# Two transformer layers on one core: merge, norm and routing of the first layer moved into attention, its operands in the weight ring's memory

## The reference, cut to what matters

```python
q, k, v = proj(Wq, bq, layernorm(x)), proj(Wk, bk, ctx), proj(Wv, bv, ctx)   # 16 heads of 16 dims, 256 positions
prob = softmax(einsum("bdhn,bdhm->bhnm", rope(q), rope(k)) / sqrt(16))
x = x + Wm @ einsum("bhnm,bdhm->bdhn", prob, v) + bm
h = layernorm(x)                                   # 1024 tokens of 256
topk_w, topk_idx = top_k(softmax(h @ gate_w.T), 8) # of 64 experts
x = x + sum over the 8 of topk_w * (silu(h @ w1[e].T) * (h @ w3[e].T)) @ w2[e].T
```

## Time and profile before

| | us |
|---|---|
| median of three runs (815.94 to 818.72) | 818.17 |
| the profiled execution's own time | 816.76 |
| its span, first to last instruction | 814.7 |
| busy: TensorE matmul, VectorE, POOL, ScalarE | 477.9, 375.1, 339.5, 206.8 |

### The profile page before, as it was taken

The page is one execution under the profiler, slowest core; times in us unless marked ns, Lnnn a source line. Parts: engine busy times, 40 slices in busy tenths (PEclk is TensorE's granted clock), DMA queues, the critical chain, the costliest instruction groups (busy, mean ns, idle before and its releaser), DMA issues. The chain is left out here.

```text
span 814.7 us, 11260 instructions
## 1 busy us (share of the span) xinstructions
PE 477.9 (59%) x3381; PEld 369.9 (45%) x3381; DVE 375.1 (46%) x1177; ACT 206.8 (25%) x533; POOL 339.5 (42%) x464
## 2 busy tenths in 40 slices
PE   2707997995645000998889920433520499898930
PEld 1602544552533000887778810322320488888820
DVE  8936766670477000343344415688760022222216
ACT  0530756675111000432223201120200122222200
POOL 8564212220047773364455440003054366666610
PEclk9965989998775555899999975655555599999975
DMA  4295478875993333799975318500007199999816
GB/s 156 75 203 111 140 227 258 248 270 180 391 365 156 155 155 126 251 320 320 325 253 173 114 56 308 221 0 20 0 21 203 42 272 289 279 301 293 255 36 254
DMA packets 78736, 159.30 MB, mean 196 GB/s; under 512 B 12267, under 2 KB 47093, under 8 KB 76896
## 3 DMA queue, kind: packets, MB, share of 16 engines
q1 hardware_dynamic: 55776, 109.72, 42.7%
q0 software_dynamic: 13168, 32.02, 11.7%
q10 hardware_dynamic: 9744, 16.98, 5.9%
HBM read 105.05 MB, written 56.12 MB: 198 GB/s over the span
## 5 line engine op out<-in xcount | busy, mean ns | idle before, releaser
L558 DVE TENSOR_REDUCE at_top<-at_ps_top 128x2 f32<-128x512 f32 x128 | 82.6, 686 | 49.2 <-PE at_ps_top L498 48.5
L1507 POOL DMA_INDIRECT rows<-hd_out,hd_rows x64 | 62.2, 972 | 66.6 <-DVE hd_out L1458 43.5
L1031 POOL DMA_INDIRECT held<-e_extended,e_address x64 | 61.9, 968 | 67.1 <-DVE e_address L1023 47.9
L1360 PE MATMUL hd_ps_up<-hd_x_turned,e_w 128*128 128x160 f32 x512 | 84.0, 308 | 0.0
L591 ACT ACTIVATE at_prob<-at_ps_score 128x512 f32<-128x512 f32 x128 | 72.2, 596 | 45.8 <-PE at_ps_score L516 45.4
L1665 PE MATMUL l_ps_up<-l_x_turned,e_up_w 128*112 128x128 f32 x672 | 82.2, 276 | 0.0
L1665 PEld LDWEIGHTS l_ps_up<-l_x_turned,e_up_w 128*112 128x112 f32 x672 | 81.0, 180 | 2.6
L1360 PEld LDWEIGHTS hd_ps_up<-hd_x_turned,e_w 128*128 128x128 f32 x512 | 77.4, 195 | 8.8 <-issue 6.2
L853 POOL DMA_INDIRECT table<-choice,ft_r_address x32 | 30.7, 958 | 111.0 <-DVE ft_r_address L844 102.2
L1495 DVE TENSOR_TENSOR hd_inner<-hd_silu,hd_ps_up 128x160 f32<-128x160 f32 x64 | 20.5, 321 | 119.5 <-ACT hd_silu L1445 118.6
L498 PE MATMUL at_ps_top<-op_k_in,op_q_in 96*128 96x256 bf16 x256 | 54.8, 302 | 23.5 <-PEq L110 21.4
(11 more groups left out here) (280 smaller groups left out, 903.6 us busy)
## 6 DMA issues: line engine op xcount, KB each, us to landing
e_w<-in_weights SPq DMA_DIRECT2D x64, 384.0 KB, 12.1
e_up_w<-in_up SPq DMA_DIRECT2D x42, 448.0 KB, 4.3
held<-at_empty ACTq DMA_DIRECT2D x16, 960.0 KB, 5.4
hd_rows<-held SPq DMA_DIRECT2D x15, 768.0 KB, 10.1
e_down_w<-in_down SPq DMA_DIRECT2D x42, 224.0 KB, 5.6
ft_g_rows<-rows SPq DMA_DIRECT2D x8, 1024.0 KB, 12.5
parts<-op_parts SPq DMA_DIRECT2D x8, 576.0 KB, 7.6
attended<-at_out SPq DMA_DIRECT2D x8, 512.0 KB, 6.4
```

The lines of the kernel that those rows point to most:

```text
L558: nc.vector.reduce_max(top[:, 2 * h:2 * h + 2], ps_top[at % TOPS][:], AX_X).then_inc(top_found, 1)
L1031: self.nc.gpsimd.indirect_dma_start(self.held_dram, to, self.held.extended[:, b, :], None)\
L1360: op = nc.tensor.matmul(ps_up[e % 2][:, part, :], w[:, k, part * P:(part + 1) * P], x_turned[g % 2][:, j, k, :], start=k == 0, stop=k == 1)
L1507: nc.gpsimd.indirect_dma_start(rows_out, to, out_ap, None, bounds_check=TOKENS * LAYER0.chosen - 1, oob_is_err=False).then_inc(semaphore, 16)
```

## The change

The merge block is gone. `attend_phase` gets its work as further steps of the pipeline: batch b's store of the second half is at step 16b + 20, read back (`load_packed`) at 16b + 22, divided at 26, merged at 27, added and normalised at 28 and 29, turned at 31, chosen at 33, ranked at 35; POOL scatters four times from 38 and four times from 46. The loop runs 28 steps past the last head. Storing and reading `attended` transposes the layout, so the sums are not turned on TensorE; the norm is applied by ScalarE. `RowRouting` works on one batch. All of merge and routing share one PSUM bank, and `at_ps_out` has one bank in place of two. `q_in`, `k_in` and `v_in` lie in an `arena` that is the weight ring's memory: ScalarE issues the 32 weight loads, one every second step from step 85, each after the batches that used its place. The emptying of `held` is issued by ScalarE in `project_phase`, 2 MB a batch, and POOL waits for all of it in attention.

```diff
--- before.py
+++ after.py
@@ Operands.__init__
-        self.q = [s.sbuf(f"q_in{n}", [ROWS, H * D], BF16) for n in range(DEEP)]
-        self.k = [s.sbuf(f"k_in{n}", [ROWS, H * D], BF16) for n in range(DEEP)]
-        self.v = s.sbuf("v_in", [P, B, 2, H, VW], F32)
+        halves = arena.bitcast(BF16)
+        self.q = [halves[0:ROWS, 2 * n * H * D:(2 * n + 1) * H * D] for n in range(DEEP)]
...
+        self.v = arena[:, DEEP * H * D:].rearrange("p (b m h v) -> p b m h v", b=B, m=2, h=H)
@@ project_phase, ScalarE, for b in range(B)
                 cut(b, full[n], 0, 3, TERMS).then_inc(high_cut, 1)
                 if b >= 1:
                     cut_mid(b - 1)
+                held.act_empty(act, b)
@@ Held
+    def act_empty(self, act, b):
+        if b == 0:
+            act.wait_ge(self.empty_set, 1)
+            act.dma_start(self.of_dummy, self.empty[:, 0:ROW0]).then_inc(self.emptied, 16)
+        each = GROUPS // B * EACH
+        act.dma_start(self.of_expert[each * b:each * (b + 1)].rearrange("e (p c) -> p e c", p=P),
+                      self.empty[:].unsqueeze(1).broadcast_to([P, each, self.PIECE])).then_inc(self.emptied, 16)
+
+    def pool_wait_emptied(self, pool):
+        pool.wait_ge(self.emptied, 16 * (B + 1))
@@ Rstd.dve_scale, in place of Norm
+        link.free(nc.vector.tensor_scalar(half, variance, EPS, -0.5, ALU.add, ALU.mult))
+        link(nc.vector.tensor_scalar(full, variance, EPS, None, ALU.add))
+        link(nc.vector.tensor_scalar(root.bitcast(I32), full.bitcast(I32), -0.5, float(0x5F3759DF), ALU.mult, ALU.add))
+        for _ in range(NEWTON):
+            link(nc.vector.scalar_tensor_tensor(work, root, half, root, ALU.mult, ALU.mult))
+            link(nc.vector.scalar_tensor_tensor(root, work, 1.5, root, ALU.add, ALU.mult))
+        nc.vector.scalar_tensor_tensor(shift, self.mean_var[:, 0:1], -1.0, root, ALU.mult, ALU.mult).then_inc(ready, 1)
@@ attend_phase, SP
+            def load_packed(b):
+                if b >= 2:
+                    sp.wait_ge(divided, b - 1)
+                for p in (2 * b, 2 * b + 1):
+                    sp.wait_ge(stored[p % 4], 16 * (p // 4 + 1))
+                by_head = attended[b].rearrange("g (j v) n -> (g j) v n", v=VW)
+                for k in range(2):
+                    sp.dma_start(packed[b % 2][:, k, :], by_head[:, k * HD:(k + 1) * HD, :]).then_inc(packed_loaded[b % 2], 16)
@@ attend_phase, POOL
+            operands.set_rows(nc, pool, DEEP - 1)
+            held.pool_wait_emptied(pool)
+            for at in range(-LEAD, END + LEAD):
+                hh, late = divmod(at + LEAD, HALF)
+                if late == HALF - 1 and hh < HALVES:
+                    cut_tops(hh)
+                for k in range(LAYER0.chosen):
+                    b = batch_at(at, SCATTER_AT + k % 4 + k // 4 * HALF)
+                    if b is not None:
+                        routing.pool_scatter(pool, b, k)
@@ attend_phase, VectorE
+            def divide(b):
+                dve.wait_ge(packed_loaded[b % 2], 32 * (b // 2 + 1))
+                link(nc.vector.reciprocal(share[:], packed[b % 2][:, 1, :]))
+                if b >= 1:
+                    dve.wait_ge(merged, b)
+                nc.vector.tensor_tensor(heads[:], packed[b % 2][:, 0, :], share[:], ALU.mult).then_inc(divided, 1)
@@ attend_phase, ScalarE
+                if at >= (DEEP + 1) * H + 4 and at % 2 == 1 and waiting:
+                    e = waiting[0]
+                    if ring.free_after[e] * H + 4 < at:
+                        act.wait_ge(weighted, 4 * ring.free_after[e])
+                        ring.load(act, waiting.pop(0))
```

More of the change, by code:

```diff
@@ new lines, in dve_targets @@
+    def dve_targets(self, dve, link, b):
+        targets = self.held.extended.bitcast(I32)[:, b, D + 1::2]
+        dve.wait_ge(self.mask_ready, b + 1)
+        link.free(self.nc.vector.tensor_tensor_scan(targets, self.consts.ones[:, 0:self.layer.experts], self.held.mask[:, b, :],
+                                                    self.consts.more[:, SLOTS_AT + b:SLOTS_AT + b + 1], ALU.mult, ALU.add))
+        dve.wait_ge(self.expo_ready, b + 1)
+        self.nc.vector.reciprocal(self.share[:], self.total[:]).then_inc(self.share_ready, 1)
@@ L1060, in pe_rows @@
         pe.wait_ge(self.own_ready, 1)
[L1061 to L1062 removed]
+        for n, to in enumerate((self.ps_row[:, 0, :], self.ps_row[:, 1, :], self.ps_block)):
+            last = self.nc.tensor.transpose(to, self.own[:, n:n + 1], self.consts.identity[:])
         last.then_inc(self.rows_ready, 1)
@@ new lines, in _ @@
+            operands.load(sp, DEEP - 1)
+            inputs.load(sp)
+            for at in range(-LEAD, END):
+                hh, late = divmod(at + LEAD - 5, HALF)
+                if late == HALF - 1 and 0 <= hh < HALVES:
+                    place(hh)
+                p, late = divmod(at - HALF - 4, HALF)
+                if late == 0 and 0 <= p < HALVES:
+                    store(p)
+                b = batch_at(at, LOAD_AT)
+                if b is not None:
+                    load_packed(b)
+                b = batch_at(at, H + 4)
+                if b is not None and b + DEEP < B:
+                    sp.wait_ge(weighted, 4 * (b + 1))
+                    operands.load(sp, b + DEEP)
@@ new lines, in weigh @@
+            def weigh(group, half):
+                b, g = group // 4, group % 4
+                if half == 0:
+                    pe.wait_ge(prob_ready, 4 * group + 4)
+                    if group >= 2 and g % 2 == 0:
+                        pe.wait_ge(out_kept, group // 2)
+                for j in range(4):
+                    last = nc.tensor.matmul(ps_out[32 * j:32 * j + VW, g % 2, :], v_in[:, b, half, 4 * g + j, :],
+                                            prob[(4 * group + j) % RING][:, half, :], start=half == 0, stop=half == 1,
+                                            skip_group_check=True)
+                if half == 1:
+                    last.then_inc(weighted, 1)
@@ new lines, in lift_once, with merge @@
+            def lift_once():
+                pe.wait_ge(inputs.loaded, 48)
+                nc.tensor.matmul(ps_merged[:, 0:1], inputs.w[:], inputs.bias[:, 0:1], start=True, stop=True).then_inc(lift_ready, 1)
+            def merge(b):
+                if b >= 1:
+                    pe.wait_ge(routing.rank_read, b)
+                else:
+                    pe.wait_ge(lift_known, 1)
+                pe.wait_ge(divided, b + 1)
+                nc.tensor.matmul(ps_merged, inputs.w[:], heads[:], start=True, stop=True).then_inc(merged, 1)
```

754 lines of the change are left out of this document (332 added, 422 removed).

## The result

The changed kernel took 845.62 us (median of 4 executions, 844.12 to 850.84), the kernel before 818.03 on the same chip: ratio 1.035, 95% interval 1.030 to 1.040. It is slower by 3.5%, where I had forecast 793. The profiled execution took 844.12 us, its span is 842.4; 791.6 had been forecast for it.

What follows compares the result with a forecast made beforehand. After attention, a merge stage waited for addresses and POOL's 81 us of scatters, while POOL and VectorE had spare time in attention. Terms -82.2 + 28 + 24 + 5 = -25 gave 791.6 profiled, median 793, range 762 to 825.

Steps and rivals of the forecast that it cites:

- VectorE's term: Attention steps 20 to 108: VectorE takes on the merge for batches 0 to 4, +24 us, bounds +3 and +40.
- Rival D: Attention: SP's placing comes late behind the half-batch's read-back and TensorE waits, +24 us, no change at 817; chance 0.11.
- my signs: Listed trace signs; wrong if emptying lands by 85, clock sits at 0.5 through a batch, or VectorE idles a quarter of middle.
- The merge stage to tail: After step 132: the 120.1 us merge stage shrinks to a 37.9 us tail for batch 7, -82.2, bounds -87 and -76.
- The emptying, +28: Projection: emptying `held` there delays POOL's first cut of the maxima and step 0 by 28 us, bounds +13 and +36.
- first cut near 98 after the last transfer: Sign at projection's end: POOL first cuts the maxima near 98 us, after the emptying's last transfer, against 70.1 before.
- ScalarE, +5: Attention steps 108 to 132: ScalarE issues 12 weight loads and does routing activations, +5 us, bounds +2 and +9.
- The reciprocal: VectorE's reciprocal of 256 values in each batch's merge, taken as 1.1 us, bounds 0.45 and 2.2.
- C: Rival: repeated TensorE stops in attention keep the clock at its lower level, granted 0.5, 844 us; chance 0.14.
- B: Rival: emptying fits in at +13, VectorE's additions fall in its waits (+3), ScalarE +2; -64, 754 us; chance 0.22.
- E: Rival: scatters don't hide in attention, needing POOL over 19 us a batch; no own chance, others together 0.03.

## Why the prediction was wrong

The forecast for the profiled execution was 791.6, the measurement 844.1, 52.5 more. Of these, 46.4 lie in the middle and late part of attention (175.3 us against 99.9 + 24 + 5 = 128.9), 4.4 in the tail and 2.6 ahead of step 20; what follows `held` took 0.6 less.

**The step that failed: VectorE's term, +24 with bounds +3 and +40.** Its sentence on waits, "nothing to 5 us a batch; I take 2, as each is one cross-engine answer issued in the same step", forgot the one wait that isn't an answer of an engine. The round trip of the attended rows was priced in the tail (9.5 us) and nowhere else, though each batch makes it, and the program gives it six steps, about 5 us. My own 9.5 against 5 leaves 4.5 a batch as soon as the two numbers stand side by side, 31 us for seven batches, and would have put the forecast at about 825, the upper end of its range; measured were 43.2 us in 7 waits, up to 12.9. They lie where the time is missing: 30.2 in the middle, which took 33.8 more than the 106.4 forecast, and 12.9 in the late part, which took 12.4 more than 22.7. With the wait covered (eight steps later) middle and late part take 132.5 us, with sixteen 130.5, where my terms, which had no such wait, gave 128.9. So their sum was right within 4 us, and the missing wait is some 43 us. That is shown, by the shifts. The 10 us of other waits and the 7 of clock loss inside the +24 were not measured one by one; of the work, add to scale took 3.1 us in the last batch and the choice 2.1 (forecast 3.0 and 2.2).

Rival D looked at the same round trip, but at SP and the placing behind it, and not at who waits for the data; it also read the 6.4 us of the earlier trace rows as the most that a store takes, where it is the median (stores and read-backs together landed after 3.0 to 9.1 us before). In the changed kernel TensorE waited 0.9 us in all for the placing, so D played no part there. VectorE was idle for over a third of the middle, which my signs had named as one of being wrong.

**The merge stage to tail, -82.2:** -77.8. Right but for the round trip, 13.1 against 9.5, just past its upper bound of 13. The rest came as forecast: from the division to the first scatter 12.4 us (11.7), scatters 10.2 (10.2), block end 6.7 (6.5).

```profile
330.87 0.96 POOL L847 DMA_INDIRECT held<-e_extended,e_address  x1 [15.64 <-DVE e_address L839]
...
340.07 0.96 POOL L847 DMA_INDIRECT held<-e_extended,e_address  x1 [0.30 <-issue]
```

That weight transfers stretch the round trip is shown by the runs that held them back (8.1 to 2.7 us from store to read-back's issue, and 6.7 to 2.2).

**The emptying, +28:** step 20 came 30.6 later. (The 28.8 us of projection's own transfers in that sum are 0.72 of the 40 us from 25 to 65.) Size right by luck, mechanism wrong: not GpSimd's wait (moving it changed nothing) but projection itself, whose transfers were slowed, up to its end at 93.1. My "first cut near 98 after the last transfer" came true at 99.4 for another reason. `parts` landed after a median of 16.7 us, against 7.6 before and 6.5 with the emptying in attention. That fits what the Trainium skill says in "DMA: Bandwidth & Descriptors", "Queues, rings and completion order", of engines that take turns between queues. The prediction had expected `parts` to land late, but not that projection's work would wait for it. Undone, this part gave back 19.6 us, not 28: projection ended some 29 us earlier, but with the transfers in attention step 20 came only 22.7 earlier.

**ScalarE, +5:** 17.4 us more in the late part, but 3.3 once the read-back is covered (21.0 against 17.7; 24.7 with sixteen steps): right, the rest belongs to the wait.

**The reciprocal:** 1.75 us for 128 x 256, taken as 1.1 (1.2 with the 0.155 of fixed cost that the sum left out), inside its bounds (2.2).

**The rivals.** C gave 844 and the time was 845.6, by chance and not for C's reason: the clock was granted at 0.84 in the middle, not 0.5, and 39 us went when the read-back was covered. B had counted on VectorE's spare 26 us; the spare time did not hide the chain, as the runs with the reciprocal twice and without division show up to the last top search. The Trainium skill's passage on waits between short bursts ("TensorE: Matmul & The Clock Gate", "HAM oscillation — how this bites in real kernels") is borne out so far, that matmuls were slower after a stop of 7 us (0.63 us for two scores against 0.38), and not so far, that the whole middle ran slow. The scatters did hide (E): 56 of 64 were done in attention.

## What to carry to other kernels

When a stage is folded into a loop, list every transfer between producer and consumer, and compare its round trip under load with the distance in steps that the program gives it; a price that is written down once at the end is otherwise missed for seven batches in the loop. An in-order engine that waits for such data stops all that is queued behind it, so the first repair is distance: one row of step numbers, which here gave back 39 us and cost nothing that the times show. And bulk transfers belong where the DMA engines have room and other engines have work: 45 us of emptying moved out of attention, where it was mostly hidden, made projection 28 us longer, and 20 us came back when it returned.

## What was not expected of the hardware

A store of 256 KB and its read-back from memory took 9.9 to 12.4 us in the changed kernel's loop and 8.1 to 17.6 in the last batch over the runs with the reciprocal on VectorE, though the least landings are 2.1 and 2.5 us. GpSimd's power of 128 x 256 f32 took 41.16 us, where VectorE's reciprocal took 1.75. With a second queue on busy DMA engines SP's own issuing was held up: 9.2 us for one operand load (0.94 at most before) and 14.1 for three stores (10.4).
